# Group norm's root packed on two sets of 64 rows, the fifth low-rank mix issued with the second decay, and the steps of all engines placed anew

## The reference

```
q = x Wq + bq;  k, v = ctx Wk + bk, ctx Wv + bv         # 32 query heads, 8 key heads of 16
x = LN((softmax(q k^T / 4 + mask) v) Wo + bo + x)
xn = LN1(x);  sx = token_shift(xn)
xxx = tanh((xn + sx * maa_x) @ maa_w1)                  # five blocks of 32
x5 = xn + sx * (maa_stack + xxx @ maa_w2)               # five mixes: w, r, k, v, g
w = exp(-exp(time_decay + tanh(x5[1] @ decay_w1) @ decay_w2))
r, k, v = x5[3] Wr^T, x5[0] Wk^T, x5[2] Wv^T;  g = silu(x5[4] Wg^T)
per token: a = k v^T;  out = r (u * a + s);  s = a + w * s     # 32 heads, 16 x 16 state
att = GroupNorm per head(out) * g;  x = x + att Wo^T
x = x + sigmoid(xr fWr^T) * (relu(xk fWk^T)^2 fWv^T)
```

## Time and profile before

| | |
|---|---|
| median of the runs | 2332.5 us |
| the profiled execution | 2330.4 us |
| its span, first to last instruction | 2328.3 us |
| TensorE (PE) busy | 2167.8 us, 93% |
| TensorE weight loads (PEld) | 1495.4 us, 64% |
| VectorE (DVE) busy | 2054.9 us, 88% |
| ScalarE (ACT) busy | 1098.5 us, 47% |
| GpSimd (POOL) busy | 613.9 us, 26% |
| mean granted TensorE clock | 0.969 of full speed, 1.00 in nearly all full periods |

### The profile page before, as it was taken

The page is one execution under the profiler, slowest core; times in us unless marked ns, Lnnn a source line. Parts: engine busy times, 40 slices in busy tenths (PEclk is TensorE's granted clock), DMA queues, the critical chain, the costliest instruction groups (busy, mean ns, idle before and its releaser), DMA issues. The chain is left out here.

```text
span 2328.3 us, 43023 instructions
## 1 busy us (share of the span) xinstructions
PE 2167.8 (93%) x14688; PEld 1495.4 (64%) x14688; DVE 2054.9 (88%) x5247; ACT 1098.5 (47%) x3765; POOL 613.9 (26%) x858
## 2 busy tenths in 40 slices
PE   3696999999999999999999999999999999999866
PEld 2474766767676676767667676766767676666533
DVE  1369999999999999999999999999999999999972
ACT  1635273644627364463727346372735536372211
POOL 1122314141232414123241412323141323313200
PEclk8898999999999999999999999999999999999877
DMA  7101001010010101001010100101010000100000
GB/s 264 41 1 42 9 11 49 11 49 1 11 49 11 49 11 49 2 11 49 11 49 11 49 1 18 42 11 49 11 49 1 29 31 11 50 2 29 1 19 9
DMA packets 48984, 69.89 MB, mean 30 GB/s; under 512 B 20512, under 2 KB 26656, under 8 KB 48768
## 3 DMA queue, kind: packets, MB, share of 16 engines
q1 hardware_dynamic: 48768, 67.15, 8.9%
HBM read 50.36 MB, written 16.78 MB: 29 GB/s over the span
## 5 line engine op out<-in xcount | busy, mean ns | idle before, releaser
L1203 DVE TENSOR_TENSOR_SCAN st<-ws,st 128x256 f32<-128x256 f32 x1024 | 646.0, 693 | 0.9 <-POOL st L1061 0.4
L859 ACT ACTIVATE probs_or_mixes<-probs_or_mixes,least 128x128 f32<-128x128 f32 x1024 | 398.7, 404 | 149.1 <-DVE least L1150 148.4
L1192 DVE TENSOR_TENSOR st<-bank_pair,kT 128x1016 f32<-128x1016 f32 x256 | 308.8, 1206 | 30.5 <-PE bank_pair L712 28.7
L1061 POOL COPY st<-s 128x8 f32<-128x8 f32 x256 | 64.0, 266 | 1015.8 <-PE bank L735 523.0
L1213 DVE TENSOR_TENSOR st<-st,rT 128x1024 f32<-128x1024 f32 x256 | 320.0, 1255 | 0.6
L1150 DVE CUSTOM_DVE_ANT_0 probs_or_mixes<-bank,nmask 128x128 f32<-128x128 f32 x1024 | 226.9, 284 | 76.9 <-POOL nmask L1049 38.2
L1085 POOL TENSOR_TENSOR probs_or_mixes<-probs_or_mixes 128x512 f32<-128x512 f32 x160 | 199.1, 1275 | 76.2 <-DVE probs_or_mixes L1263 76.2
L859 ACT ACTIVATION_READ_ACCUMULATOR probs_or_mixes<-probs_or_mixes,least 128x1 f32 x1024 | 207.4, 203 | 0.0
L1091 POOL TENSOR_TENSOR rstd<-rstd,mhalf 128x1 f32<-128x1 f32 x96 | 80.1, 834 | 442.9 <-DVE rstd L1234 442.9
L712 PE MATMUL bank_pair<-v_hi,sel 32*128 32x256 f32 x1024 | 183.2, 340 | 13.6 <-DVE st L1192 13.6
L565 PE MATMUL bank<-kbd,inputs_turned 32*128 32x256 f32 x1024 | 148.6, 400 | 29.9 <-DVE least L1150 25.8
(11 more groups left out here) (146 smaller groups left out, 4178.9 us busy)
## 6 DMA issues: line engine op xcount, KB each, us to landing
inputs_turned<-in_ctx_turned SPq DMA_DIRECT2D x16, 512.0 KB, 3.6
inputs_turned<-in_x_turned SPq DMA_DIRECT2D x16, 512.0 KB, 4.7
xin<-in_x SPq DMA_DIRECT2D x16, 512.0 KB, 3.8
x<-xin SPq DMA_DIRECT2D x16, 512.0 KB, 4.0
keep<-x SPq DMA_DIRECT2D x16, 512.0 KB, 3.5
out<-keep SPq DMA_DIRECT2D x32, 256.0 KB, 2.0
...
```

The source lines that it names most:

```text
L859: last = fn(pr[:, n % 4, j, :], pr[:, n % 4, j, :], ACT.Exp, bias=least[:, n, j:j + 1], scale=-1.0, accum_out=rsum[:, n, j:j + 1])
L1192: tt(dst, src, over(kv, DU, 1), ALU.mult).then_inc(outer.sem, 1)
L1203: last = nc.vector.tensor_tensor_scan(v, ws[:, c].rearrange("p b t -> p (b t)"), v, 0.0, ALU.mult, ALU.add)
```

## The change

1. The root's tile is 128 columns wide (TQ = T // 2): chunk c and half q of the columns on rows 32c + 8q to 32c + 8q + 7. `var` issues 8 matmuls of 128 columns in place of 16 of 64, Newton's operations are 128 columns wide, and `rstd` issues 8 matmuls that contract over 64 rows in place of 16 over 32 rows. The wait between the two halves of `rstd` goes.
2. `low_rank.4` is gone. `decay.1` issues mix 4 with the decay: contraction over rows 64 to 127 of `low_b` and `low2`, whose last 32 rows are filled with zeroes by GpSimd at the start. `flip` writes a tile of its own in place of rows 96 to 127 of `low_b`.
3. All four lists are new. The weight row of the group norm is 64 KB larger.

```diff
-TQ = T // 4
+TQ = T // 2
...
-low_rank.0+1 reduce.5+2 key.0 spread.13+2 tdecay.0+1 low_rank.2+1 spread.14+2 proj_r.0+1 spread.15+2 decay.0+1
-proj_v.0+1 proj_k.0+1 spread.0+1 decay.1+1 reduce.6+2 low_rank.4+1 reduce.7+2 spread.1+1 query.0 var.0+2 spread.2+1
-score.0 proj_r.1+1 query.1 spread.3+1 rstd.0+2 proj_g.0+1 proj_g.1+1 score.2 value.0 reduce.0+1 spread.4+1 turn_p.0
-turn_p.1 turn_p.2 score.4 spread.5+1 out.0+2 turn_p.3 score.6 values.0 reduce.1+1 turn_p.4 turn_p.5 out.1+2
-spread.6+1 score.8 proj_v.1+1 flip.0 turn_p.6 proj_k.1+1 turn_p.7 turn_m.0+2 score.10 spread.7+1 values.1 turn_p.8
-turn_p.9 score.12 spread.8+1 share.0 turn_p.10 reduce.2+1 score.14 turn_p.11 project.0 turn_m.1+2 values.2 turn_p.12
-turn_p.13 spread.9+1 reduce.3+1 flip.1 turn_p.14 turn_p.15 spread.10+1 share.1 values.3 ffn_k.0+2 project.1 ffn_k.1+2
-spread.11+1 ffn_r.0+2 ffn_r.1+2 turn_n.0 turn_n.1 ffn_v.0+2 ffn_v.1+2 low.0 reduce.4+1 spread.12+1
+low.0+1 spread.12+2 reduce.4+2 low_rank.0+1 reduce.5+2 spread.13+2 key.0 tdecay.0+1 low_rank.2+1 spread.14+2
+proj_r.0+1 spread.15+2 decay.0+1 proj_v.0+1 proj_k.0+1 spread.0+1 reduce.6+2 decay.1+1 reduce.7+2 spread.1+1 query.0
+spread.2+1 var.0+2 score.0 proj_r.1+1 spread.3+1 query.1 rstd.0+2 proj_g.0+1 spread.4+1 proj_g.1+1 score.2 value.0
+reduce.0+1 turn_p.0 turn_p.1 turn_p.2 score.4 out.0+2 turn_p.3 reduce.1+1 score.6 spread.5+1 values.0 turn_p.4
+out.1+2 spread.6+1 score.8 turn_p.5 proj_v.1+1 turn_p.6 flip.0 proj_k.1+1 turn_p.7 turn_m.0+2 spread.7+1 score.10
+values.1 share.0 turn_p.8 turn_p.9 turn_p.10 spread.8+1 score.12 reduce.2+1 score.14 turn_p.11 project.0 turn_m.1+2
+values.2 spread.9+1 turn_p.12 flip.1 reduce.3+1 turn_p.13 turn_p.14 turn_p.15 share.1 spread.10+1 values.3 ffn_k.0+2
+project.1 spread.11+1 ffn_k.1+2 ffn_r.0+2 ffn_r.1+2 turn_n.0 turn_n.1 ffn_v.0+2 ffn_v.1+2
...
 ACT_ORDER, the steps that the prediction names
-... proj_v.1+1 turn_p.6 apply2.0+2 flip.0 score.9 apply2.1+2 row0.0 proj_k.1+1 ...
+... share.1 ffn_k.0+2 row0.0 keep_row.0 apply0.1 state.0 apply1.0 ffn_k.1+2 ffn_r.0+2 apply1.1 ffn_r.1+2 turn_n.0 row1.0 turn_n.1 state.1
...
 POOL_ORDER
-affine0.0+1 first.10+2 norm0.1+1 ... first.0+1 first.1+1 negate.0 rk.0+1 ... first.8+1 bias.0 bias.1 first.9+1 norm0.0
+mix.3+1 first.0+1 first.1+1 rk.0+1 bias.0 negate.0 first.2+1 first.3+1 mix.4+1 first.4+1 bias.1 ...
...
 DVE_ORDER
-... weigh.6+1 scan.8+1 weigh.7+1 inverse.1 project.0
-outer.9+1 shift2.0+2 norm0.0 gather.1 scan.9+1 outer.10+1 project.1 norm0.1 norm1.0 weigh.8+1 outer.11+1 weigh.9+1
-norm1.1 readout.1+1 scan.10+1 weigh.10+1 shift.0 scan.11+1 ffn_v.0+2 ffn_v.1+2 weigh.11+1 outer.12+1 mix.0 mix.1
-readout.2+1 outer.13+1 scan.12+1 mix.2 mix.3 outer.14+1 weigh.12+1 outer.15+1 scan.13+1 scan.14+1 proj_v.0 weigh.13+1
+weigh.6+1 weigh.7+1 project.0 inverse.1 norm0.0 outer.9+1 shift2.0+2 readout.1+1 outer.10+1 gather.1 scan.8+1
+scan.9+1 project.1 norm0.1 norm1.0 weigh.8+1 outer.11+1 norm1.1 weigh.9+1 scan.10+1 weigh.10+1 shift.0 scan.11+1
+ffn_v.0+2 weigh.11+1 ffn_v.1+2 mix.0 outer.12+1 mix.1 readout.2+1 outer.13+1 scan.12+1 mix.2 mix.3 outer.14+1
...
+        elif name == "decay":
+            keys = [("decay", n)] + [("mix", 8 + m) for m in range(2 * n)]
...
             def decay(g, p):
-                ps, full = x_bank(("decay", p), g, through("tdecay", 0))
+                keys = [("decay", p)] + [("mix", 8 + m) for m in range(2 * p)]
+                banks = [x_bank(key, g, through("tdecay", 0)) for key in keys]
+
+                def low_mm(m, q):
+                    ps, full = banks[m]
+                    r = slice(0, DEC) if m == 0 else slice(DEC, P)
+                    c = 2 * (p if m == 0 else m - 1) + q
+                    last = mm(ps[:, q * T:(q + 1) * T], low2[r, c * P:(c + 1) * P], low_b[r, :], start=True, stop=True)
+                    if q == 1:
+                        last.then_inc(full, 1)
+
                 for q in range(2):
-                    c = 2 * p + q
-                    last = mm(ps[:, q * T:(q + 1) * T], low2[0:DEC, c * P:(c + 1) * P], low_b[0:DEC, :],
-                              start=True, stop=True)
-                last.then_inc(full, 1)
+                    for m in range(p + 1):
+                        low_mm(m, q)
+                if p == 1:
+                    for q in range(2):
+                        low_mm(2, q)
...
                 for m in range(2):
-                    if m == 1:
-                        pe.wait_ge(half_rstd.sem, half_rstd.after(g, 2))
-                    for q in range(4):
-                        for c in (m, m + 2):
+                    for q in range(2):
+                        for p in range(2):
                             o = m * T + q * TQ
-                            last = mm(ps[c // 2][0][:, o:o + TQ], bsel[32 * c:32 * c + 32, q, :],
-                                      y[32 * c:32 * c + 32, :], start=True, stop=True)
-                            if q == 3:
-                                last.then_inc(half_rstd.sem if m == 0 else ps[c // 2][1], 1)
+                            r = slice(64 * p, 64 * p + 64)
+                            last = mm(ps[p][0][:, o:o + TQ], bsel[r, m, q, :], y[r, :], start=True, stop=True)
+                            if m == 1 and q == 1:
+                                last.then_inc(ps[p][1], 1)
...
             def flip(g, b):
-                ps, free = x_full(("flip", b), g, through("share", b, back=1))
-                fn(low_b[96:128, b * L:(b + 1) * L], ps[96:128, 0:L], ACT.Copy).then_inc(free, 1)
+                ps, free = x_full(("flip", b), g, through("share", 0) if b else through("share", 1, back=1))
+                fn(flipped[96:128, :], ps[96:128, 0:L], ACT.Copy).then_inc(free, 1)
...
+            for n, tile in enumerate((low_b, low2)):
+                nc.gpsimd.memset(tile[96:128, :], 0.0).then_inc(zeroed, 1)
+                pool.wait_ge(zeroed, 2 + n)
```

More of the change, by code:

```diff
@@ L137 @@
-score.12 score.13 score.14 turn_p.11 score.15 turn_m.1+2 turn_p.12 turn_p.13 flip.1 turn_p.14 turn_p.15 share.1
-apply0.0 ffn_k.0+2 apply0.1 state.0 ffn_k.1+2 ffn_r.0+2 row1.0 apply1.0 keep_row.0 apply1.1 turn_n.0 turn_n.1
-square.0+1 ffn_r.1+2
+square.0+2 low.0+1 key.0 tdecay.0+1 decay.0+1 proj_r.0+1 proj_v.0+1 row2.0+2 proj_k.0+1 decay.1+1 square.1+2 query.0
+score.0 score.1 proj_r.1+1 query.1 proj_g.0+1 proj_g.1+1 score.2 turn_p.0 turn_p.1 turn_p.2 score.3 state.2+1 score.4
+turn_p.3 score.5 score.6 turn_p.4 state.3+1 score.7 turn_p.5 apply2.0+2 score.8 flip.0 apply2.1+2 turn_p.6 proj_v.1+1
@@ L140 @@
+score.9 proj_k.1+1 turn_p.7 turn_m.0+2 score.10 turn_p.8 share.0 score.11 turn_p.9 turn_p.10 score.12 score.13
+turn_p.11 score.14 score.15 turn_m.1+2 turn_p.12 flip.1 turn_p.13 turn_p.14 turn_p.15 apply0.0 share.1 ffn_k.0+2
+row0.0 keep_row.0 apply0.1 state.0 apply1.0 ffn_k.1+2 ffn_r.0+2 apply1.1 ffn_r.1+2 turn_n.0 row1.0 turn_n.1 state.1
 """
 POOL_ORDER = """
-affine0.0+1 first.10+2 norm0.1+1 first.11+2 norm1.0+1 affine0.1+1 norm1.1+1 first.12+2 first.13+2 rk.3+2 mix.0+1
-mix.1+1 mix.2+1 mix.3+1 first.14+2 first.15+2 first.0+1 first.1+1 negate.0 rk.0+1 first.2+1 mix.4+1 first.3+1
@@ L145 @@
-first.4+1 first.5+1 rk.1+1 first.6+1 norm2.0+2 norm2.1+2 rk.2+1 first.7+1 first.8+1 bias.0 bias.1 first.9+1 norm0.0
+mix.3+1 first.0+1 first.1+1 rk.0+1 bias.0 negate.0 first.2+1 first.3+1 mix.4+1 first.4+1 bias.1 first.5+1 rk.1+1
+norm2.0+2 first.6+1 first.7+1 norm2.1+2 first.8+1 first.9+1 rk.2+1 norm0.0 first.10+1 first.11+1 affine0.0 norm0.1
+norm1.0 affine0.1 norm1.1 first.12+1 first.13+1 rk.3+1 mix.0 first.14+1 first.15+1 mix.1 mix.2
 """
 DVE_ORDER = """
-weigh.14+2 weigh.15+2 outer.0+1 mix.4+1 readout.3+2 outer.1+1 scan.0+1 var.0+2 score.0 score.1 weigh.0+1 outer.2+1
@@ L155 @@
-norm1.1 readout.1+1 scan.10+1 weigh.10+1 shift.0 scan.11+1 ffn_v.0+2 ffn_v.1+2 weigh.11+1 outer.12+1 mix.0 mix.1
-readout.2+1 outer.13+1 scan.12+1 mix.2 mix.3 outer.14+1 weigh.12+1 outer.15+1 scan.13+1 scan.14+1 proj_v.0 weigh.13+1
-scan.15+1
+outer.15+2 weigh.13+2 proj_v.0+1 scan.15+2 weigh.14+2 weigh.15+2 outer.0+1 mix.4+1 outer.1+1 readout.3+2 scan.0+1
+outer.2+1 score.0 score.1 weigh.0+1 var.0+2 scan.1+1 outer.3+1 groupnorm.0+2 scan.2+1 proj_g.0+1 weigh.1+1 scan.3+1
+score.2 proj_g.1+1 score.3 value.0 weigh.2+1 outer.4+1 weigh.3+1 score.4 score.5 scan.4+1 out.0+2 score.6 outer.5+1
@@ new lines @@
+score.7 scan.5+1 norm2.0+2 out.1+2 score.8 outer.6+1 score.9 norm2.1+2 inverse.0 weigh.4+1 readout.0+1 weigh.5+1
+proj_v.1+1 scan.6+1 score.10 score.11 outer.7+1 scan.7+1 score.12 gather.0 score.13 outer.8+1 score.14 score.15
+weigh.6+1 weigh.7+1 project.0 inverse.1 norm0.0 outer.9+1 shift2.0+2 readout.1+1 outer.10+1 gather.1 scan.8+1
+scan.9+1 project.1 norm0.1 norm1.0 weigh.8+1 outer.11+1 norm1.1 weigh.9+1 scan.10+1 weigh.10+1 shift.0 scan.11+1
+ffn_v.0+2 weigh.11+1 ffn_v.1+2 mix.0 outer.12+1 mix.1 readout.2+1 outer.13+1 scan.12+1 mix.2 mix.3 outer.14+1
@@ L158 @@
+weigh.12+1 scan.13+1 scan.14+1
 """
@@ L644, in low_rank @@
```

(15 more changed lines are left out.)

28 lines of the change are left out of this document (11 added, 17 removed).

## The result

The changed kernel takes 2355.1 us (2353.6 to 2356.6) against 2332.5 us before: ratio 1.0097, 95% interval 1.0080 to 1.0115. It is 22.6 us slower, in the forecast's direction and range, but more than double its 10.5 us.

A forecast was written before the change was run, and what follows sets the result against it. TensorE was taken as the bound by a hair, VectorE close behind. 15 periods x 0.7 us plus 0.2 for start and end made +10.7 us, a median of 2343 us, range 2317 to 2358.

The forecast's parts named there:

- the chain at the turn: Turn of the period: spread.12 alone delays low_rank.0, VectorE waits about 1.4 us at mix.0; +0.7 us a period.
- rival C: TensorE: two 64-row tiles don't pair; period 137.3 us, time 2369 us; chance 7%.
- Newton: VectorE: twelve operations go from 64 to 128 columns, +0.75 us a group.
- `row0`'s move: ScalarE: row0 goes behind ffn_k.0, context load L402 leaves about 27 us later; costed at nothing.
- Rival A: Faster: end costs not paid again where the queue is full, VectorE's waits close; period 133.5, 2311 us; chance 17%.
- Rival D: VectorE late at the scores holds up ScalarE's exponentials and TensorE's turns; 0.8 us more a period, 2355 us; chance 13%.
- TensorE's sum: TensorE per group: mix -0.87, root -0.76, changes of tile shape +1.4, lost overlap +0.14; sum -0.1 us.
- The new places: TensorE's order: seven more changes of tile shape a period, at 0.19 to 0.21 us each, +1.4 us.
- the lost overlap: TensorE: spread.12 and low_rank.0 no longer stand together, +0.14 us.
- the chain's second half: After mix.0: mix.1 to mix.3 come about 1.2 us later, and proj_r.0's idle time becomes about 1 us.
- the start: Before the first score: bias.0 ahead of the negated mask +1.25 us, 64 KB more of weights +0.2.
- The end: Last group's root: half of its 32 passes go, -2.0 us, and the wider VectorE operations give back 0.75.

The follow-up runs named there:

- parts_old_order: The changed kernel with all four lists of steps as before, low_rank.4 taken out of TensorE's: 2318.7 us, ratio 0.9944.
- new_order_only: The kernel before, without the two parts, with the four new lists of steps: 2376.3 us, ratio 1.0188.
- spread12_back: The changed kernel with TensorE issuing spread.12 directly before low_rank.0, as before: 2345.8 us, ratio 1.0055.
- spreads_back: The kernel with the turn restored, with TensorE's spread.2, spread.3 and spread.4 back in their places of before: 2340.0 us, ratio 1.0036.
- bias_later: The changed kernel with GpSimd's bias.0 directly behind negate.0 in place of ahead of it: 2355.7 us, ratio 1.0099.
- the turn restored: The changed kernel with outer.12 before mix.0, spread.12 directly before low_rank.0 and spread.13 behind key.0, as before: 2341.4 us, ratio 1.0041.
- root_later: parts_old_order with GpSimd's affine0.1 ahead of norm1.0: 2303.2 us, ratio 0.9882.
- three_engines_back: spreads_back with VectorE's var.0 ahead of score.0, GpSimd's affine0.1 ahead of norm1.0 and ScalarE's proj_r.1 ahead of score.1: 2331.9 us, ratio 1.0005.

## Why the prediction was right or wrong

**Right.** The order loses time and the parts gain it, and the chain at the turn is where I had it: `mix.0` waits 1.3 us for `low_rank.0` (forecast 1.4), `norm1.1` 2.1 us (2.3), `spread.12` alone takes 0.67 us. The merged step takes 2.0 us (1.9) and refutes rival C. The root's step takes 1.09 us (1.04) and 2.08 us at the end in place of 4.04, as forecast. Newton gives back 0.61 us (0.75). `row0`'s move sends the context load L402 31 us ahead of the next `key.0` in place of 56, and nothing waits for it. Rival A is refuted by TensorE's busy time, 133.1 us. Rival D's time, 2355, came out, but VectorE's waits at the scores (L1156) are 0.7 us, where they were 1.0: its mechanism is not the one.

**Wrong: TensorE's sum, -0.1 us a period, measured +0.6.** This is the larger part of the miss. Two terms were off. The parts gave 1.4 to 1.5 us (`parts_old_order`, and the changed kernel against `new_order_only`), where mix, root and one change of shape fewer made 0.87 + 0.76 + 0.2 = 1.83. Each part is some 0.15 us short: the mix alone gave 1.10 us of busy time, where 0.87 and its two changes made 1.27 (the merged step takes 2.00 us, where the recorded costs make 1.93), and the root alone gave 0.41, where 0.76 less its one new change made 0.56. The new places cost 2.0 to 2.1 us, where 8 changes at 0.2 and the lost overlap made 1.74. Over the kernels that ran at full clock, busy time is 131.0 at 55 changes, 132.0 at 58, 132.5 at 61 and 133.1 at 63 with the parts, and 132.5 at 56 and 134.6 at 64 without: 0.26 us a change, the lost overlaps included. The price by itself rests on two runs that move nothing else on TensorE: `spread12_back` (0.56 us for two changes) and `spreads_back` (0.55 us for three). It isn't one number for all places: by the same reckoning the two changes that go with the mix are worth 0.1 us each.

**Wrong: the chain's second half.** `proj_r.0` was to wait 1 us for `mix.2`; it does not wait. I followed VectorE's delay into the mixes and not into `outer.12`, whose banks `spread.13` needs. With `spread.13` moved ahead of `key.0`, eight passes of cover are gone, and TensorE waits 1.1 us there. What stands behind a waiting step waits with it, and I had not followed it further. The forecast's idle time was +0.8 us a period (0.7 + 0.1) and measured +1.2 (3.4 against 2.2 in the means at full clock), so this step is off in place more than in size. Together with the 0.7 us above, and less 0.1 for the slower period before, that is 1.0 us a period, 13 us over 13 periods.

**Wrong: the start, measured +5.8 in the profiled executions.** I priced +1.45 us for it and 0.7 for each of its two early periods, 2.85 us in all. Why it took twice that stays open. The first score is 1.8 us later than before (51.1 against 49.4), of which 1.2 us are the bias. The second `key.0` is 4.4 us later (122.96 against 118.55), and between them the granted clock differs from execution to execution, as in `bias_later`. The third starts at 246.2 with the turn restored and at 244.2 with the spreads back, which speaks for the order; but with the old order and both parts it starts at 246.6, 2.8 us later than before, which the order can't explain. The end gave 2.4 us back (1.25), and the difference of the medians, 22.6 us, is 2.8 us below that of the profiled executions. So that the whole is off by 12 us and not by 15 is chance.

**What stays open.** The best version in the new order, 135.0 us, is 1.9 us a period behind `root_later`. TensorE's busy time is 1.0 us of it, the wait that moved from place to place 0.85. Which of VectorE's steps holds that stretch was not found. One lead is in the traces: VectorE is busy 129.3 us a period there and 127.7 in `root_later` with the same steps, and its `scan`s are 1.1 us of the difference. GpSimd's and VectorE's timelines of `three_engines_back` show four scans that take 3.49 us beside GpSimd's `mix` and 2.43 without it:
```profile
1083.85 2.32 POOL L1088 TENSOR_TENSOR probs_or_mixes<-probs_or_mixes 128x512 f32<-128x512 f32 x2
```
```profile
1084.97 3.49 DVE L1210 TENSOR_TENSOR_SCAN st<-ws,st 128x256 f32<-128x256 f32 x4
...
1106.32 2.43 DVE L1210 TENSOR_TENSOR_SCAN st<-ws,st 128x256 f32<-128x256 f32 x4
```
The first four stand ahead of the wait for VectorE's gate in the same period, in the stretch that was late. So where GpSimd's list puts its mixes is a rival to the order of VectorE's own steps, and no run separates the two.
